# A graph network in one kernel: the second GAT layer from a count matrix instead of edge gathers

## The reference, cut to what matters

```python
feat = (h @ fc_w.T).reshape(n, heads, out_dim)      # heads = 1, out_dim = 128
el, er = einsum(feat, attn_l), einsum(feat, attn_r)
e = leaky_relu(el[src] + er[dst], 0.2)
m = segment_max(e, dst)
ex = exp(e - m[dst])
alpha = ex / segment_sum(ex, dst)[dst]
out = segment_sum(alpha * feat[src], dst) + h @ res_w.T + bias
```

## Time and profile before

| | us |
|---|---|
| median of 3 runs | 2798.61 (2792.72 to 2805.59) |
| the profiled execution's own time | 2798.99 |
| its span, first to last instruction | 2796.3 |
| PE busy | 1962.9 (70%) |
| PE weight loads | 1362.9 (49%) |
| DVE busy | 1395.3 (50%) |
| POOL busy | 1381.5 (49%) |
| ACT busy | 964.2 (34%) |

### The profile page before, as it was taken

One profiled execution on the slowest core, in us unless ns is written; L12 is line 12 of the kernel. 1 busy time (PEld: TensorE's weight loads), 2 busy tenths in 40 slices (PEclk: granted clock), 3 DMA queues, 4 the chain that ended last, 5 costly groups with the idle time before them and its releaser, 6 DMA issues.

```text
span 2796.3 us, 33506 instructions
## 1 busy us (share of the span) xinstructions
PE 1962.9 (70%) x10867; PEld 1362.9 (49%) x10867; DVE 1395.3 (50%) x3099; ACT 964.2 (34%) x2148; POOL 1381.5 (49%) x1417
## 2 busy tenths in 40 slices
PE   3288896498888885557777776844444445499998
PEld 2155664377777773433333333533333334266666
DVE  7588857377777765544444443422222223522414
ACT  3444424233333335634444442422222222301202
POOL 5000004677777754677777770567777773300000
PEclk9998998689999886778888886865555555799999
DMA  4678892589999961167777773335555553565461
GB/s 105 188 277 300 278 312 75 169 251 262 265 259 275 259 197 42 29 190 240 239 240 243 238 233 106 74 78 133 133 133 133 133 133 82 187 204 155 142 202 31
DMA packets 469164, 505.22 MB, mean 181 GB/s; under 512 B 103669, under 2 KB 426632, under 8 KB 467552
## 3 DMA queue, kind: packets, MB, share of 16 engines
q1 hardware_dynamic: 245740, 211.11, 25.8%
q10 hardware_dynamic: 172724, 176.76, 19.3%
q0 software_dynamic: 50528, 115.22, 16.5%
HBM read 288.69 MB, written 227.42 MB: 185 GB/s over the span
## 4 chain that ended last, share of the span: by engine, by line
POOL 39%; PE 22%; issue 16%; DVE 12%; DMA 8%; ACT 3%; SPq 0%; POOLq 0%; ACTq 0%; DVEq 0%
POOL arena L1041 35%; PE ps L1603 10%; DVE arena L2013 3%; DMA arena<-erank 3%; PE ps L1585 2%; PE ps L1696 2%; PE ps L1491 1%; PE ps L1874 1%; DMA arena<-edst,step_i 1%; POOL arena L968 1%; DMA arena<-t_attn,src_i 1%; PE ps L1722 1%; DVE arena L2483 1%; ACT arena L1072 1%; DVE same_b L2159 1%
## 5 line engine op out<-in xcount | busy, mean ns | idle before, releaser
L1072 ACT ACTIVATE arena<-ps 128x774 f32<-128x774 f32 (+8 forms) x689 | 492.8, 729 | 1146.2 <-PE ps L1696 652.1
L1041 POOL DMA_INDIRECT arena<-t_gat,src_i x784 | 740.5, 944 | 238.9 <-issue 236.8
L1696 PE MATMUL ps<-arena 128*128 128x136 f32 (+2 forms) x2352 | 691.3, 455 | 86.4 <-DVE arena L2373 83.5
L1696 PEld LDWEIGHTS ps<-arena 128*128 128x128 f32 x2352 | 462.6, 260 | 237.3 <-DVE arena L2373 117.0
L1041 POOL DMA_INDIRECT arena<-t_attn,src_i x392 | 382.4, 975 | 126.5 <-issue 113.9
L2321 DVE TENSOR_TENSOR z_b<-arena 128x12 f32<-128x12 f32 (+1 forms) x196 | 33.6, 171 | 595.4 <-DMA arena<-t_gat,src_i 588.1
L1603 PE MATMUL ps<-arena 128*128 128x384 bf16 x1850 | 305.0, 328 | 35.0 <-DVE rec L2530 32.5
L1654 PE MATMUL ps<-ident,logit 128*64 128x128 f32 (+2 forms) x147 | 48.2, 328 | 381.2 <-DVE logit L2334 313.3
L1603 PEld LDWEIGHTS ps<-arena 128*128 128x128 bf16 x1850 | 181.8, 98 | 158.0 <-issue 40.6
L2373 DVE TENSOR_TENSOR arena<-arena,ps 128x1536 f32<-128x1536 f32 (+1 forms) x196 | 229.9, 1215 | 1.6 <-ACT arena L1231 1.6
L1654 PEld LDWEIGHTS ps<-ident,logit 128*64 128x64 f32 (+2 forms) x147 | 14.2, 97 | 427.0 <-DVE logit L2334 353.7
(11 more groups left out here) (323 smaller groups left out, 2579.2 us busy)
## 6 DMA issues: line engine op xcount, KB each, us to landing
ends_gat<-arena ACTq DMA_DIRECT2D x98, 774.0 KB
arena<-adj_hbm SPq DMA_DIRECT2D x90, 640.0 KB, 3.9
same_b<-same_hbm SPq DMA_DIRECT2D x294, 128.0 KB, 4.7
adj_hbm<-arena ACTq DMA_DIRECT2D x9, 3200.0 KB, 11.4
ends_attn<-arena ACTq DMA_DIRECT2D x98, 272.0 KB
ends_gat<-arena ACTq DMA_DIRECT2D x98, 258.0 KB
arena<-starts_q SPq DMA_DIRECT2D x98, 256.0 KB, 5.3
same_hbm<-same_b SPq DMA_DIRECT2D x98, 128.0 KB, 3.8
```

What stands on the lines that cost most here:

```text
L1041: g.indirect_dma_start(out=row_b[:, n % RB, k, 0:row_tab[p].shape[1]], out_offset=None, in_=row_tab[p], in_offset=bass.IndirectOffsetOnAxi ...
L1072: return a.activation(o, i, ACT.Copy)
L1696: i = mm(o, same_f[:, g % RB, k, :], msg[:, g % 4, k * W:(k + 1) * W], start=True, stop=True)
```

## The change

The edge pass of gat2 goes, with its table store, its scatter, its zero fill and the gathers of results. In its place `feat` and a column of ones are kept in `tab_gat1` (129 columns), and the chunks of the count matrix are read back, the narrow one first (`CHUNKS`), into two buffers, five pieces each. For each chunk i and source tile t the weights are made for all pairs that the block of counts holds:

- First, for the chunk after the current one, DVE's `look` runs over the 25 tiles: min of count and a scaled el (in 0 to 1, so an absent pair gives 0), then max with the running result. PE turns it, DVE's `maxima2` reduces it and gives m and two columns per target: 0.8 er, and 0.2 er - m. PE spreads each over the partitions by a product with the identity (`rows_a`, `rows_b`), ACT and DVE copy them (`row_kept`, `row_copied`).
- Then per tile: ACT Relu(row_a + 0.8 el), POOL adds row_b, ACT Exp(. + 0.2 el) into PSUM, DVE caps it and multiplies by the counts (`w_b`), PE adds `w_b` times the 129 columns of the table in f32, four products for a wide tile. `taken` copies the sums of a finished chunk.
- In the last chunk's loop DVE also works out factors that join steps of one target with different maxima (`pens`, `merged`, two scans over 1184 columns) and the selection in f32 (`select2`). After it: scaling (`scaled`), denominators and rows by f32 selection on PE, turning back, and reciprocal, product and residual in one step per tile. The node stage starts at xad.

er of the targets comes by ten indirect gathers (`er_g`) from a table that ACT now stores. The diff, cut:

```diff
@@ SP
-            for j in range(NJ):
-                sp.wait_ge(feat_out, TURNS[j][1])
-                store_row(node_rows(row_tab["gat2"], j), tiles(tab_gat1, j))
-                store_row(node_rows(er_tab["gat2"], j), tiles(er_all["gat2"], j))
-            edge_pass("gat2")
+            for i in range(NC):
+                if i < 2:
+                    sp.wait_ge(pe_o.sem, pe_o.at("gat1", ("tr", "lin")[i]))
+                for q in range(NT // PIECE2):
+                    if i >= 2:
+                        sp.wait_ge(*w_done.at((i - 2) * NT + ((q + 1) * PIECE2 if i > 2 else NT)))
+                    load_piece(i, q)
-            sp.wait_ge(s_steps, chains["x_gat2"].end)
+            sp.wait_ge(pe_o.sem, pe_o.at("gat2", "tr"))
@@ POOL
-                scatter("gat2", j)
-            edge_pass("gat2")
+            for ch in CHUNKS:
+                g.indirect_dma_start(out=er_g[:, ch, :], out_offset=None,
...
+            for n in range(NC * NT):
+                i = n // NT
+                if n % NT == 0:
+                    pool.wait_ge(*dve_2.at("row_b", i))
+                pool.wait_ge(*relu2_done.at(n + 1))
+                z = log_b[:, n % 4, 0:wide(i)]
+                gt(z, z, row_b2[:, i % 2, 0:wide(i)], ALU.add).then_inc(sum2_done.sem, 1)
@@ ACT
+            def relus(n):
...
+                if n >= 4:
+                    act.wait_ge(*exp2_done.at(n - 3))
+                a.activation(log_b[:, n % 4, 0:wide(i)], row_a[:, i % 2, 0:wide(i)], ACT.Relu, bias=el8[:, t:t + 1])                    .then_inc(relu2_done.sem, 1)
+            def exps2(n):
...
+                act.wait_ge(*sum2_done.at(n + 1))
+                if n >= 3:
+                    act.wait_ge(*w_done.at(n - 2))
+                a.activation(bank((2, 4, 0)[n % 3])[:, 0:wide(i)], log_b[:, n % 4, 0:wide(i)], ACT.Exp,
+                             bias=el2[:, t:t + 1]).then_inc(exp2_done.sem, 1)
+            for n in range(NC * NT + 2):
+                if n % NT == 12 and n // NT < NC - 1:
+                    row_kept(n // NT + 1)
+                if n < NC * NT:
+                    relus(n)
+                if n >= 2:
+                    exps2(n - 2)
@@ PE
+            def products(i, t):
+                n = i * NT + t
+                pe.wait_ge(*w_done.at(n + 1))
...
+                for dl in range(wide(i) // P):
+                    m = mm(out2(i, dl), part(w_b[:, n % 3, :], dl), tab_gat1[:, t, :], start=t == 0 and dl in (0, DG - 1),
+                           stop=t == NT - 1, skip_group_check=True)
+                m.then_inc(out2_done.sem, 1)
...
+                    products(i, t)
+                    if i < NC - 1:
+                        if t == 6:
+                            rows_a(i + 1)
+                        elif t == LOOK_BY - 2:
+                            look_turned(i + 1)
+                        elif t == LOOK_BY:
+                            rows_b(i + 1)
@@ DVE
+            def look(i, t):
...
+                    k = stt(acc[:, 0:w], adj2_of(i, t), y_el[:, t:t + 1], acc[:, 0:w], ALU.min, ALU.max)
+                k.then_inc(look_done.sem, 1)
...
+                    if i < NC - 1 and t < LOOK_BY:
+                        for k in range(t * NT // LOOK_BY, (t + 1) * NT // LOOK_BY):
+                            look(i + 1, k)
+                    if t == 2 and i >= 1:
+                        taken(i - 1)
+                    dve.wait_ge(*exp2_done.at(n + 1))
...
+                    if n >= 3:
+                        dve.wait_ge(*out2_done.at(n - 2))
+                    stt(w_b[:, n % 3, 0:wide(i)], bank((2, 4, 0)[n % 3])[:, 0:wide(i)], TOP, adj2_of(i, t), ALU.min, ALU.mult)                        .then_inc(w_done.sem, 1)
+                    if i < NC - 1:
+                        if t == LOOK_BY + 2:
+                            maxima2(i + 1)
+                        elif t == LOOK_BY + 5:
+                            row_copied(i + 1)
...
+                    elif t == 7:
+                        pens()
+                    elif t == 12:
+                        merged()
+                    elif 14 <= t < 19:
+                        select2(2 * (t - 14), 2 * (t - 13))
@@ DVE, the node stage
-            in_turns(dve_o, "gat2", **weighted("gat2"),
-                     yr=by_turn(dve_o, "gat2", "num", lambda j: tiles(agg_of("gat2"), j)[:, :, 0:D],
+            in_turns(dve_o, "gat2", xad=added,
```

More of the change, by code:

```diff
@@ L34 @@
 UNROLL = 4
[L35 removed]
+WEIGHTED = {"attn": (H1, C1, 0.25), "gat1": (H2, D, 1.0)}
 PASSES = tuple(WEIGHTED)
@@ L67 @@
 RING = 9
+CHUNKS = [NC - 1] + list(range(NC - 1))
+PIECE2 = 5
+ONE = D + 1
+LOOK_BY = 17
+TOP = 1.0e30
 SAME0 = 20
@@ new lines, in rows_a, with look_turned @@
+            def rows_a(i):
+                pe.wait_ge(*dve_2.at("er9" if i == 0 else "er"))
+                if i >= 1:
+                    pe.wait_ge(*dve_2.at("row_b", i - 1))
+                spread_rows(i, r_a[:, CHUNKS[i], :], pe_2.sem)
+            def look_turned(i):
+                pe.wait_ge(*look_done.at((i + 1) * NT))
+                pe.wait_ge(*act_2.at("row_a", i))
+                for dl in range(wide(i) // P):
+                    m = nc.tensor.transpose(part(bank(1), dl), part(acc, dl), ident[:, :])
+                m.then_inc(pe_2.sem, 1)
@@ new lines, in factors @@
+            def factors():
+                pe.wait_ge(*act_2.at("f"))
+                pe.wait_ge(*dve_2.at("fg"))
+                for ch in range(NC - 1):
+                    nc.tensor.transpose(bank(1)[:, ch * DG:(ch + 1) * DG], part(m_r, ch), ident[0:DG, 0:DG])
+                mm(bank(1)[:, (NC - 1) * DG:(NC - 1) * DG + 1], f_g[:, :, :].rearrange("d e s -> d (e s)"), ones[0:DG, 0:1],
+                   start=True, stop=True).then_inc(pe_2.sem, 1)
+            rows_a(0)
+            look_turned(0)
@@ new lines, in den_turned @@
+            def den_turned():
+                pe.wait_ge(*dve_2.at("tiny"))
+                for t in range(NT):
+                    k = min(P, NGRP * DG - t * P)
+                    m = mm(bank(7)[0:k, t:t + 1], by_dl2[:, :, :].rearrange("d g e -> d (g e)")[:, t * P:t * P + k],
+                           ones[0:DG, 0:1], start=True, stop=True)
+                m.then_inc(pe_2.sem, 1)
+            pe.wait_ge(*dve_2.at("sel"))
+            pe.wait_ge(*dve_2.at("s_v"))
+            denominators()
@@ new lines, in _ @@
+            settled()
+            ts(dg[0:2, :], ident[0:2, 0:2], lim[0:2, 0:1], None, ALU.mult).then_inc(dve_2.sem, 1)
+            dve.wait_ge(*pe_2.at("sum"))
+            did(v.tensor_copy(c2[:, :], bank(1)[:, 0:2]))
+            settled()
+            did(tt(rng[:, :], c2[:, 0:1], c2[:, 1:2], ALU.add))
+            settled()
+            did(ts(inv[:, :], rng[:, :], 1.0 / TOP, None, ALU.max))
+            settled()
+            did(v.reciprocal(inv[:, :], inv[:, :]))
+            settled()
@@ L2592, in split1 @@
+            settled()
+            for j in range(NJ):
+                dve.wait_ge(pe_o.sem, pe_o.at("gat2", "tr", j))
+                for k, t in enumerate(range(*TURNS[j])):
+                    i = stt(y_gat2[:, t, :], part(bank(j), k), rec2[:, t:t + 1], h_sb[:, t, :], ALU.mult, ALU.add)
+                i.then_inc(y2_done.sem, 1)
             def split1(stage, after):
```

365 lines of the change are left out of this document (345 added, 20 removed).

## The result

The changed kernel takes **2837.98 us** (median of four runs, 2832.72 to 2840.48) against 2802.1 for the kernel before beside it: ratio 1.0134, 95% interval 1.0118 to 1.0150. It is slower by 1.3%; the forecast was 2780 and faster. The profiled execution took 2838.61 us for a span of 2836.9, so its trace stands for the median.

What follows compares the result with a forecast made beforehand. POOL issuing gathers was taken as the bound, a stage of 588.5 us. New terms 20 + 30 + 4 + 392 (eight chunks of 49) + 41 + 83 = 570 gave 2780 us, range 2725 to 2840.

Steps and rivals of the forecast that it cites:

- Lead-in: From the last table copy to the first weights: chained short ops, narrow looks and first maximum, 20 us.
- narrow chunk: The first chunk, 128 columns wide, with looks for the first wide chunk: 30 us, before 4 for a load.
- tail: Behind the last weights: scaling, denominators and rows by selection, turning back, reciprocal steps; 83 us together.
- look stretch: Weights 0 to 16 of a wide chunk, where DVE's looks alternate with POOL's adds: 39 us plus 0.5.
- no lead: Rival, chance 0.15: POOL never gets ahead, look, add, Exp and weights run in a row; 64 per chunk, 2900, half 2840.
- The eight tiles without looks: Rest of a wide chunk, weights 17 to 24 with the maximum and row copy: 9.5 us at the high clock.
- Four chained ones at 0.22: DVE's maximum for the next chunk: one step of 0.68 us and four short ones at 0.22, 1.56 together.
- The port: POOL's add and a DVE instruction with both inputs in SBUF exclude each other: 1.68 us for an add and a look.
- 0.86 for rows and 0.95 for tile 18 before w_b is free: PE's work after the maximum: row broadcast, then tile 18's products, before a weight buffer is free for weights 21.
- The last chunk: Wide chunk without looks: POOL's adds 34 us, DVE's merging, penalties and selection 19, partly covered by buffers; 41 us.
- clock rival: Rival, chance 0.13: PE stays at the low clock and its f32 products cost 54 us per chunk, 2820.
- cheap port: Rival, chance 0.12: POOL's adds mostly run beside DVE's weights or short steps; a chunk takes 38 us, 2692.

Runs made afterwards that it cites:

- narrow_add: The changed kernel with POOL adding 4 columns of a tile instead of all 512 (or 128), all instructions kept: 2683.07 us, ratio 0.9591.
- rows_b_later: The changed kernel with PE's broadcast of r_b two products later in its order (behind product 19, not 17): 2808.05 us, ratio 1.0028.
- whole_chain_psum: rows_b_later, with each chained-maximum step reading at most one SBUF tensor (two more copies) and four last-chunk TENSOR_SCALARs moved to before the first row copy: 2790.3 us, 0.9971.
- maximum_earlier: The changed kernel with DVE's chained maximum two tiles earlier and the row copied behind weights 20 instead of 22: 2808.11 us, ratio 1.0027.
- half_products: The changed kernel without two of the four f32 products of tiles 1 to 23 in the eight wide chunks before the last: 2831.5 us, 1.0127.
- both_in_psum: look_in_psum, with each chained-maximum step reading at most one SBUF tensor and four last-chunk TENSOR_SCALARs moved to before the first row copy: 2692.2 us, ratio 0.9618.
- no_looks: The changed kernel without 24 of the 25 looks of each wide chunk after the second, chain and row kept: 2689.46 us, ratio 0.9616.
- chain_in_psum: rows_b_later, with the first steps of the chained maximum keeping their four columns in PSUM: 2805.59 us, ratio 1.0025.
- look_in_psum: rows_b_later, with the looks' running maximum kept in a PSUM bank and two banks for Exp in place of three: 2722.15 us, ratio 0.9733.

## Why the prediction was wrong

**What held.** The gathers went; the unchanged rest kept its 367.3 us. Lead-in, narrow chunk, load wait and tail came within 2.4 us each of their sums. The look stretch, worked out from the earlier trace rows as pairs of add and look, was 40.3 for 39.5, and the free-port pitch of 38 that stood as the lower end was 37.3 in narrow_add. Of the marks named for it these hold: the add at 1.49 on average and 1.56 where looks run (2057 to 2096 us), weights 0.68, look above 1. The pitch of 46 to 52 does not. First weights came at 1859.2 for 1860. The last (2383.5 for 2327) and the end of the stage (2469.6 for 2410) carry the miss. Slips in its arithmetic are small beside it: the earlier trace rows give 5.9 us and not 5.3 for the two scans (measured 6.1), the terms behind the last weights add up to 83.6, and those of no lead to 63.2 and not 64.

**The step that failed** is "The eight tiles without looks", 9.5 us, measured 14.5: 5 x 8 = 40 of the 60.9 us. It has two parts. "Four chained ones at 0.22" took that price from a stretch with no POOL instruction beside it, although stood next to it. The paragraph "The port" gave the exclusion to the look alone; the chain runs beside adds too, one step of two SBUF tensors and one TENSOR_SCALAR, and was held up by 2.1 us (1.38 + 1.19 - 2 x 0.22); the steps behind them met no add. Worked against rows_b_later, whole_chain_psum shows 1.5 of that net of its copies. The other part is PE: "0.86 for rows and 0.95 for tile 18 before w_b is free" was 1.55 + 3.04, both at a clock below full (0.66 from 2103 to 2108 us), with two tiles of products behind the broadcast rather than one. rows_b_later shows 3.7 for having it in that place. The stretch with looks takes 40.1 us in rows_b_later and 40.0 in whole_chain_psum; taken off the pitches, that leaves 10.8 and 9.4 us without looks, so with both parts mended the prediction's 9.5 is met. The other 0.8 of a chunk's miss is in the stretch with looks.

**The last chunk**, 41, measured 52.2. The same omission: the selection (4) and the penalties (4.5) were priced free of the port, and the TENSOR_SCALARs of both took 2.2 to 4.5 times as long. narrow_add, without the port, has 40.4. Of the 11.8 us between them 9.1 are DVE instructions that became shorter: 3.3 in L2969, 0.9 in L2985, 3.9 in the nine of L2995 (807 to 374 ns on average) and 1.1 in L3001. The other 2.7 are less waiting of DVE for Exp and PE (9.8 to 7.1 us). Whether those are the port too is not shown, since narrow_add also took most of POOL's own time out of the stretch.

**The rivals.** No lead gave 2840 for half of the tiles, and the time came out at 2838, but by another way. That was luck: maximum_earlier gave POOL all the lead and only 3.6 us per chunk, which rows_b_later got without it. Its marking point, 53 us per chunk, was passed; the measurement lies in the range (2725 to 2840), which this rival had stretched, for the wrong reason. The clock rival had 54 per chunk and 2820, and its sign came true: of the 44.5 us that the weights waited, 35.4 were for PE. Its mechanism did not: rows_b_later took 22 of 23.9 us of that wait away (1900 to 2300 us) with the clock at the same 0.77, and with 41% fewer records a chunk was 0.7 us shorter. The prediction had weighed what the Trainium skill tells ("TensorE: Matmul & The Clock Gate", section "A second HAM failure mode"), a clock that goes back and forth at the cost of throughput. The runs do not show such a cost as the pace here: in half_products the clock fell from 0.77 to 0.61 and the pitch fell as well. In both_in_psum, where DVE waits less and PE has the same products to do in less time, the granted clock was 1.00. The cheap port is the opposite of what ran, and that its number, 2692, is the time of both_in_psum is luck in part: that kernel takes the accumulator and the chain off the port, and it has PE's order mended too.

**The direction** turned on 18.5 us of gain in a sum with 60.9 of miss: both errors, of a few us each, were multiplied by eight chunks.

## What to carry to other kernels

Once a trace shows that two engines exclude each other, apply it to every instruction of the one that runs beside the other, the four-column steps above all: whatever its size, such an instruction waits for the other engine's. Two steps of four columns lost about 1 us each to POOL's adds in the changed kernel (1.37 for 0.31 and 1.18 for 0.16), and in no_looks one of them lost 3.3 us, to all the adds that POOL had left in its chunk. Keep a running result that is read and written by every step in PSUM if a bank can be had; it took 10.6 us off a chunk of 50.9. And an in-order engine should reach an operation that waits for a long chain only after all the work that is already ready: two products moved ahead of the broadcast were worth 1.1%.

## What the runs showed of the hardware that was not expected

- A TENSOR_SCALAR with one SBUF tensor and pointers is held up by POOL's add like an instruction with two: 1161 ns against 307 (four columns), 1192 against 472 (518 columns), in the changed kernel and in narrow_add. With tensor and result in PSUM it is not: 290 in chain_in_psum.
- The wait is not bounded by one instruction of the other engine. In no_looks, where POOL's adds of 1.28 us came without a gap, the four-column TENSOR_SCALAR took 3.61 to 3.65 us in seven chunks of eight and ended 0.02 to 0.03 us after POOL's last add of the chunk. Why it was let in after one add in the changed kernel (1.37 us) is open.
- The first look of a chunk, a TENSOR_SCALAR of 512 bf16 columns, takes 0.48 us from SBUF to SBUF in narrow_add (0.52 in the changed kernel) and 0.75 into PSUM: undisturbed, SBUF is the faster place for it, and beside an add (1.58 in rows_b_later) the slower.
- Less work on PE went with a lower clock: 820 records in 350 us at 0.61 (half_products), 1398 at 0.77, and 909 in 150 us at 1.00 (both_in_psum). The number alone does not set it: from 1950 to 2200 us no_looks had 1465 records at 0.91, look_in_psum 1366 at 0.97.
